# Softmax of the local attention layers: masked scores exponentiated tile by tile and head by head on ScalarE, with norm, maximum and sum inside the instruction, and new instruction orders on every engine

## What is computed

```python
for i in range(DEPTH):                       # 6 layers
    x = attn_layer(shift_tokens(x), Wqkv[i], q_scale[i], k_scale[i], Wo[i]) + x
    x = ffn_layer(shift_tokens(x), ...) + x
# attn_layer: 16 heads of 64
q = l2norm(q) * qs ; k = l2norm(k) * ksc     # then rotary positions, with a scale by position
# local_attention: windows of 32 queries look at 64 keys (their own window and the one before)
sim = jnp.einsum('bhwie,bhwje->bhwij', bq, bk2) * QK_SCALE
sim = jnp.where(mask, -jnp.finfo(sim.dtype).max, sim)
attn = jax.nn.softmax(sim, -1)
out = jnp.einsum('bhwij,bhwje->bhwie', attn, bv2)
```

## Time and profile before

| | |
|---|---|
| median of 3 runs | 3527.9 us (3526.22 to 3528.53) |
| the profiled execution's own time | 3527.28 us |
| its span, first to last instruction | 3525.5 us |
| mean granted clock of TensorE | 0.977 of full speed |
| busy: TensorE / VectorE / GpSimd / ScalarE | 3293.5 / 2843.1 / 2640.0 / 1832.3 us |

### The profile page before, as it was taken

How to read it: one execution, slowest core, us unless ns; L and a number is a source line. 1 busy time by engine, 2 the same in 40 slices (tenths; PEclk the granted TensorE clock), 3 DMA queues, 4 the chain that set the end, 5 groups by cost and what they waited for, 6 DMA issues and landing times. The chain is left out here.

```text
span 3525.5 us, 69882 instructions
## 1 busy us (share of the span) xinstructions
PE 3293.5 (93%) x26940; PEld 1611.1 (46%) x26940; DVE 2843.1 (81%) x3289; ACT 1832.3 (52%) x2692; POOL 2640.0 (75%) x1918
## 2 busy tenths in 40 slices
PE   5788876899999999999999999999999999999986
PEld 3222222454555545454545455555555454545443
DVE  5788846888888888888888888888888888888862
ACT  2477772454545454555555555555454545455532
POOL 3133206998888888888888888888888888888850
PEclk7799998999999999999999999999999999999998
DMA  6232214333333323333323333333333233333211
GB/s 209 73 63 48 47 37 113 79 73 73 71 86 79 80 71 72 83 71 82 78 71 79 79 81 77 73 73 85 83 74 79 68 78 78 83 77 71 71 46 49
DMA packets 178233, 270.01 MB, mean 77 GB/s; under 512 B 42481, under 2 KB 67185, under 8 KB 176241
## 3 DMA queue, kind: packets, MB, share of 16 engines
q1 hardware_dynamic: 174160, 251.10, 29.6%
q10 hardware_dynamic: 3744, 14.43, 1.1%
HBM read 44.49 MB, written 19.55 MB: 18 GB/s over the span
## 5 line engine op out<-in xcount | busy, mean ns | idle before, releaser
L1084 DVE SCALAR_TENSOR_TENSOR ly_prod<-ly_pj_ps,ly_few,ly_tables 128x1024 f32<-128x1024 f32 x768 | 964.6, 1272 | 190.1 <-ACT ly_sq L1216 165.5
L1216 ACT ACTIVATE ly_sq<-ly_pj_ps 128x512 f32<-128x512 f32 x768 | 451.0, 601 | 745.8 <-PE ly_pj_ps L918 702.7
L918 PE MATMUL ly_pj_ps<-ly_xs,ly_wqk 128*128 128x512 f32 x1536 | 796.1, 616 | 35.2 <-DVE ly_prod L1084 22.5
L999 PE MATMUL ly_to_ps<-ly_u,ly_mvo 128*128 128x512 f32 x1536 | 720.6, 598 | 0.1
L1325 POOL TENSOR_TENSOR ly_sq<-ly_sq 128x512 f32<-128x512 f32 x384 | 491.6, 1280 | 220.0 <-ACT ly_sq L1216 219.8
L1247 ACT COPY ly_u<-ly_pair_ps 128x1024 f32<-128x1024 f32 x384 | 378.7, 1013 | 240.6 <-PE ly_pair_ps L987 240.6
L1329 POOL TENSOR_TENSOR ly_sx<-ly_sx,ly_smax 128x1024 f32<-128x1024 f32 x192 | 366.2, 1907 | 145.3 <-DVE ly_smax L1124 145.3
L918 PEld LDWEIGHTS ly_pj_ps<-ly_xs,ly_wqk 128*128 128x128 f32 x1536 | 269.2, 191 | 426.4 <-issue 291.5
L999 PEld LDWEIGHTS ly_to_ps<-ly_u,ly_mvo 128*128 128x128 f32 x1536 | 277.1, 190 | 287.2 <-issue 287.2
L987 PE MATMUL ly_pair_ps<-ly_pt,ly_xt 32*128 32x512 f32 x3072 | 385.3, 615 | 19.9 <-ACT ly_u L1247 13.0
L967 PE MATMUL ly_pair_ps<-ly_kbd,ly_qp 128*32 128x128 f32 x12288 | 374.7, 276 | 22.2 <-DMA ly_kbd<-ly_kr 18.9
(11 more groups left out here) (113 smaller groups left out, 4317.5 us busy)
## 6 DMA issues: line engine op xcount, KB each, us to landing
ly_qp<-ly_qr SPq DMA_DIRECT2D x768, 128.0 KB, 2.3
ly_kbd<-ly_kr SPq DMA_DIRECT2D x1536, 64.0 KB, 2.0
ga_parts_dram<-ga_parts SPq DMA_DIRECT2D x16, 384.0 KB, 2.3
ga_qs<-ga_parts_dram SPq DMA_DIRECT2D x96, 64.0 KB
ga_ks<-ga_parts_dram SPq DMA_DIRECT2D x96, 64.0 KB
ly_wqk<-in_wqk SPq DMA_DIRECT2D x24, 256.0 KB, 4.0
ly_mvo<-mvo_dram SPq DMA_DIRECT2D x6, 1024.0 KB, 6.4
mvo_dram<-ga_pt ACTq DMA_DIRECT2D x4, 1024.0 KB, 4.0
```

The lines of the kernel that those rows point to most:

```text
L918: pe.matmul(pj_ps[:, j % 2, :], wqk[:, g, j % TILES, :], xs[:, n % 2, WIN:], start=True, stop=True).then_inc(proj_ready.sem, 1)
L999: last = pe.matmul(to_ps[:], mvo[:, h, :], u[:, :, :, h, :].rearrange("p t c q -> p (t c) q"), start=(h == 0), stop=(h == LH - 1))
L1084: dve.scalar_tensor_tensor(prod[:, k], pj_ps[:, j % 2, :].unsqueeze(1).to_broadcast([P, 2, N]), gains[:, n // B, k:k + 1], tables[:, table ...
L1216: act.activation(sq[:, k, :], pj_ps[:, j % 2, :], ACT.Square).then_inc(sq_done.sem, 1)
```

## The change

In the stack's softmax, `less_max` and `scale_scores` on GpSimd and the row sums on VectorE are gone. In their place VectorE computes `less` = -maximum x inverse norm of the query (16 columns a unit, `maxima_off`), and ScalarE computes exp(score x inverse norm + less) with the inverse norm as the instruction's scale and `less` as its bias. Both are one value per token and head, so the unit's one instruction becomes 16, for four tiles by four heads, of 64 columns each; each also writes out its row sum (`accum_out`). `exponentials(n, k)` now counts in tiles: k = 4g + t. The orders of all five engines' bodies are written anew, and the bodies run to `ITEMS + 5` in place of `ITEMS + 6`.

```diff
-            for i in range(-1, ITEMS + 6):
+            for i in range(-1, ITEMS + 5):
...
+            def maxima_off(n, g):
+                dve.wait_ge(s_max.sem, s_max.at(n, g + 1))
+                dve.wait_ge(steps.sem, steps.at(n, STEPS))
+                if UNITS * n + g >= 2:
+                    dve.wait_ge(p_exp.sem, T * (UNITS * n + g - 1))
+                rq = rn[:, n % 2, 0:NSUM].rearrange("p (t r) -> p t r", t=T)[:, :, 4 * g:4 * g + 4]
+                dve.scalar_tensor_tensor(less[:, g % 2], smax[:, g % 2], -1.0, rq, ALU.mult, ALU.mult).then_inc(s_less.sem, 1)
+
             def prob_sums(n, g):
-                dve.wait_ge(p_exp.sem, p_exp.at(n, g + 1))
-                if UNITS * n + g >= 2:
-                    dve.wait_ge(p_ready.sem, UNITS * n + g - 1)
-                dve.tensor_reduce(rsum[:, g % 2], sx[:, g % 2], AX.X, ALU.add).then_inc(p_sum.sem, 1)
-                dve.wait_ge(p_sum.sem, p_sum.at(n, 2 * g + 1))
+                dve.wait_ge(p_exp.sem, p_exp.at(n, T * g + T))
                 dve.reciprocal(rsum[:, g % 2], rsum[:, g % 2]).then_inc(p_sum.sem, 1)
...
-            def exponentials(n, g):
-                act.wait_ge(s_scaled.sem, s_scaled.at(n, g + 1))
-                act.activation(sx[:, g % 2], sx[:, g % 2], ACT.Exp).then_inc(p_exp.sem, 1)
+            def exponentials(n, *parts):
+                for k in parts:
+                    g, t = k // T, k % T
+                    act.wait_ge(s_less.sem, s_less.at(n, g + 1))
+                    if t == 0 and UNITS * n + g >= 2:
+                        act.wait_ge(p_ready.sem, UNITS * n + g - 1)
+                    for h in range(4):
+                        rq = 2 * LH * t + 4 * g + h
+                        last = act.activation(sx[:, g % 2, t, h], sx[:, g % 2, t, h], ACT.Exp, bias=less[:, g % 2, t, h:h + 1],
+                                              scale=rn[:, n % 2, rq:rq + 1], accum_out=rsum[:, g % 2, t, h:h + 1])
+                    last.then_inc(p_exp.sem, 1)
...
-            def less_max(n, g):
-                pool.wait_ge(s_max.sem, s_max.at(n, g + 1))
-                pool.tensor_tensor(sx[:, g % 2], sx[:, g % 2], smax[:, g % 2].unsqueeze(3).to_broadcast([P, T, 4, SPAN]),
-                                   ALU.subtract).then_inc(s_less.sem, 1)
-
-            def scale_scores(n, g):
...
```

More of the change, by code:

```diff
@@ L813, in bodies @@
         def bodies(body):
-            for i in range(-1, ITEMS + 6):
-                body(i, known(i + 1), *(known(i - k) for k in range(7)))
+            for i in range(-1, ITEMS + 5):
+                body(i, known(i + 1), *(known(i - k) for k in range(6)))
         @block.sync
@@ L1060, in body @@
                 if x_5 is not None: up(x_5, 2)
-                if x_2 is not None: scores(x_2, 2); scores(x_2, 3)
+                if x_2 is not None: scores(x_2, 2)
                 if x_1 is not None: square_sums(x_1, 3)
@@ L1067, in body @@
                 if x_3 is not None: combine(x_3, 0, 1)
+                if x_2 is not None: scores(x_2, 3)
+                if x_3 is not None: combine(x_3, 2, 3)
+                if x_1 is not None: spread_norms(x_1, 0)
+                if x_3 is not None: combine(x_3, 4)
             bodies(body)
@@ L1170, in body @@
-                if x_1 is not None: products(x_1, 10, 11)
+                if x_1 is not None: products(x_1, 9, 10, 11)
                 if x_5 is not None: gated(x_5, 1)
-                if x_2 is not None: scale_keys(x_2, 3)
+                if x_2 is not None: scale_keys(x_2, 2); scale_keys(x_2, 3)
                 if x_1 is not None: products(x_1, 12, 13)
-                if x_2 is not None: prob_blocks(x_2, 0)
+                if x_2 is not None: prob_sums(x_2, 0); score_maxima(x_2, 1); maxima_off(x_2, 1); prob_blocks(x_2, 0)
@@ L1180, in body @@
-                norms(i - 1)
-                if x_2 is not None: prob_blocks(x_2, 1); mask_scores(x_2, 3)
+                if x_2 is not None: maxima_off(x_2, 2)
+                if x_1 is not None: scale_keys(x_1, 0); products(x_1, 15)
+                if x_2 is not None: prob_blocks(x_2, 1)
                 if x_0 is not None: products(x_0, 0)
-                if x_2 is not None: score_maxima(x_2, 3)
-                if x_1 is not None: scale_keys(x_1, 0)
-                if x_0 is not None: products(x_0, 1)
```

162 lines of the change are left out of this document (79 added, 83 removed).

## The result

The changed kernel is slower: 3681.1 us (median of 4 runs, 3680.2 to 3691.2) against 3527.1 us for the kernel before on the same chip, ratio 1.0442, 95% interval [1.0428, 1.0456]. The prediction, 3507 us with a range of 3482 to 3620, was wrong in sign and in range. The profiled execution took 3691.2 us, 10 above the median, its span 3689.4.

The account below looks back on a forecast made before the run. TensorE was taken to bound the steady bodies, with ScalarE just fitting. From 3527.3 us, 44 bodies at 0.2 us less gave 9 us and the fill 11, so 3507 us; own range 3495 to 3519, 8-in-10 range 3482 to 3620.

Parts of the forecast that it names:

- A head costs 390 ns: ScalarE: each 64-column exponential with scale, bias and sum takes 350 to 470 ns, taken as 390; 25.0 us an item.
- The rival: ScalarE takes over: the sum is its own instruction, a head 450 to 470 ns; chance 0.19, 0.14 for about 430.
- The slope beyond 405 ns, 8+32 heads: Steady body: beyond about 405 ns a head, 40 heads lie on the path; 10 ns more cost 0.4 us an item.
- Rooms of 0.1 and of 0.2 to 0.5 us: ScalarE's slack against TensorE at 390 ns a head: 0.1 us in stretch 1, 0.2 to 0.5 us in stretch 2.
- stretch 1: Attend 3 to the copy of the sums: ScalarE needs 9.55 us including 8 heads, TensorE needs the copy after 9.67.
- stretch 2: Spread_norms 0 to attend 0, with 32 heads: ScalarE's path about 18.8 us, TensorE's work 19.0 to 19.3 us.
- A body of 59.96 us as the base: Steady stage: one TensorE body of 59.96 us was to fall 0.2 to 59.75, 9 us less over 44 bodies.
- Place of the loss: If slower: stretch 2, TensorE idle ahead of attend 0, waiting for the last unit's transposed probabilities, released by VectorE's transpose.
- The new wait at attend 3: TensorE: attend 3 waits about 0.4 us for the PSUM slot scale_keys 3 frees, one projection after spread_norms 3.
- the rival that doubled them: ScalarE's table loads hold the engine twice as long as their row, some 2.6 us an item: 3617 us; chance 0.02.
- Fill, 11 us less: Pipeline filling: without GpSimd's passes the third body takes 50 us, 7 less; second and fourth 2 less each; 4 to 16.
- Drain, none, 5 either way: Pipeline draining: a unit's chain goes from 11.9 to 12.3 us, taken as no change, 5 us either way.

Follow-up runs that it names:

- e3: Changed kernel with one exponential of 256 columns per tile, constant scale, no bias and no row sums: 3549.1 us, body 60.69 us.
- e9: e3 with square_sums 2 and spread_norms 3 moved ahead of projection 12 on TensorE: 3536.1 us, body 60.23 us.
- e4: Changed kernel with Tanh in place of Gelu in the gates, so no tables are loaded in the stack: 3646.7 us, body 62.48 us.
- e15: Kernel before, without VectorE's row maxima and GpSimd's pass that subtracts them: 3523.1 us, ratio 0.9995.

## Why the prediction was wrong

- **A head costs 390 ns: failed, and the first cause.** It is 425 ns: 333 for the exponential with scale and bias, 92 for reading the sum. The term had 350 and 40. The bounds of 350 to 470 held, the choice between them didn't. The reason given, "one value is written, not 64 columns", is what failed: the one value is an instruction of its own, of 192 ns, half hidden. The rival named this sign, and the page shows it.
- **The slope beyond 405 ns, 8+32 heads: too flat by itself.** At 425 ns it gives 40 x 20 ns = 0.8 us a body, 60.55 us and a time near 3542. Measured: 63.26. The missing 2.7 us are two terms. The orders' own cost took 0.94 (e3's 60.69 against the 59.75 forecast). The rooms took the other 1.77.
- **Rooms of 0.1 and of 0.2 to 0.5 us: failed, and the larger cause.** They were busy times set against each other to 0.1 us. ScalarE's sides were right: at 425 ns stretch 1 comes to 9.83 us (measured 9.88) and stretch 2 to 19.9 (measured 19.94, from the widening at 2004.22 to attend 0). TensorE's were too long: in e3 it needs the copied sums 9.51 us after its projection, not 9.67, and reaches attend 0 18.8 us after the spreading, not 19.0 to 19.3. So there was no room in either: stretch 1 is 0.5 late where 0.2 would follow, and attend 0 another 1.26 where 0.6 to 0.9 would. The 0.7 us behind attend 0 were in no term: 0.52 stand ahead of attend 1, where TensorE waits for a product that VectorE makes behind the last unit's transpose, and 0.20 at attend 2.
- **A body of 59.96 us as the base: an error in the sum.** It was one body; 44 of them had been read as 59.81 on average. From there to 59.75 is 0.06 us, 3 us in 44 and not 9, so the same terms give 3513 us.
- **Place of the loss: right as a stretch, wrong as a wait.** The text looked for it ahead of attend 0, released by VectorE's transpose. TensorE waits for GpSimd's sum of squares ahead of it and for products behind it. The other sign, a wait for the copied sums, is there with 0.36 us.
- **The new wait at attend 3: right, undersized.** 0.4 us expected, 0.61 in the trace; e9 shows that 0.46 of it costs. That the gaps saved elsewhere would make the body 59.75 failed: a second new wait, 0.4 us for VectorE's product ahead of attend 1, wasn't seen.
- **Table loads: right.** Four an item (126 in the window), 1283 ns each, the next instruction 1.29 us after the start. Removing them all gives 0.78 us (e4), so the rival that doubled them had no ground. The Trainium skill's switch of 2.66 us (ScalarE: Activation LUTs, What ACT_TABLE_LOAD costs) again appears in no row.
- **ScalarE's 55.2 us: 56.7 measured.** The heads' 64 x 35 ns are 2.2 us more, all the rest together 0.7 less.
- **Fill, 11 us less: failed.** It is 1.9 longer, which is no difference by its spread. GpSimd's third body did fall to 37.6 us (expected 40), but in e15, where it falls by 7.8 us and nothing is added elsewhere, the fill is 1.4 us shorter. So the step "with GpSimd's passes gone the third body takes 50" mistook an engine that was busy for one that paced. With a light ScalarE and the new orders the fill gains 4 to 8 us (e3, e9). In the changed kernel the wait of the earlier trace rows for masking is replaced by one for ScalarE's widening:

```profile
624.70 0.75 PE L957 MATMUL ly_pair_ps<-ly_ident,ly_rnx 128*128 128x128 f32 x4 [3.47 <-ACT ly_rnx L1237]
```

- **Drain, none, 5 either way: failed**, 13 more. The chain of a unit was costed at 6.2 us for its heads plus 0.25 for the bias; the last two items' attend 0 wait 3.8 and 4.5 us for the transposed probabilities where only the last waited, 1.8 us, and ScalarE's other work stands between the heads. The clock has a part that no run separates. It is 0.92 from the last of the `down` groups counted to the last of all, 0.98 before and 0.99 in e3, and it falls behind these two waits, where an attend takes 3.54 and 3.69 us for its 2.00. The estimate from above is 0.08 of 151.6 us less 0.02 of 138.7, 9 of the 13 us. The window and TensorE's timeline:

```profile
3511.01:3662.58 151.57, 123.29 (x707) 59.31 (x704) 57.93 (x104) 87.58 (x274) 19.18 (x12) 0.92 0.09 22
```

```profile
3540.38 3.54 PE L988 MATMUL ly_pair_ps<-ly_pt,ly_xt 32*128 32x512 f32 x16 [3.81 <-DVE ly_pt L1146]
```

- **GpSimd and VectorE hidden in the steady stage: right.** e15 shows it for half of GpSimd's 15.2 us: no body is shorter.
- **The chances.** The slow side had 0.35, and its two cases named the right instruction; their prices, 3545 at 430 ns and 3615 at 470, were below 3681 because they took the same rooms and the same cost of the orders, and nothing behind attend 0.
